# Graph network and experts on one core: the first graph layer's order, and its residual summed on TensorE

## The reference

```python
xn = layernorm(x)                                   # [3125, 256]
e = leaky_relu(el[src] + er[dst])                   # 4 heads
alpha = softmax of e over the edges of one dst
rst = segment_sum(feat_src[src] * alpha, dst) + gat_bias
h = xn + elu(rst)
graph = relu(h @ w1 + b1) @ w2 + b2                 # 256 -> 512 -> 256
mix = linear attention of xn, @ W_out + b_out
x = x + graph + mix
x = x + experts(layernorm(x), router fed with the mean over all nodes)
```

## Time and profile before

| | |
|---|---|
| runs | 2421.73, 2429.51, 2425.75 us, median 2425.75 |
| the profiled execution's own time | 2447.78 us, 0.9% over that median |
| its span in the trace | 2446.1 us |
| mean granted TensorE clock | 0.787 |
| busy in the span: PE, PEld | 1618.2, 1285.4 us |
| DVE, ACT, POOL | 1311.2, 777.3, 1128.7 us |
| most costly groups | L460 gathers 437.1 us, L1084 matmuls 330.8 us, L1020 scalings 323.0 us |

### The profile page before, as it was taken

How to read it: one execution, slowest core, us unless ns; L and a number is a source line. 1 busy time by engine, 2 the same in 40 slices (tenths; PEclk the granted TensorE clock), 3 DMA queues, 4 the chain that set the end, 5 groups by cost and what they waited for, 6 DMA issues and landing times. The chain is left out here.

```text
span 2446.1 us, 31537 instructions
## 1 busy us (share of the span) xinstructions
PE 1618.2 (66%) x8029; PEld 1285.4 (53%) x8029; DVE 1311.2 (54%) x4007; ACT 777.3 (32%) x2662; POOL 1128.7 (46%) x1255
## 2 busy tenths in 40 slices
PE   4534656655667579699897456677666666676593
PEld 3433434433344368588886335555555455565592
DVE  4722655665567758566766154444444444466344
ACT  2211744563356623256664101100100000122251
POOL 2762666666663013221213555555555555526441
PEclk8755676776668879899998687778888777787796
DMA  4751434343432073354442322222222222222586
GB/s 150 208 165 53 110 105 116 108 116 103 120 99 64 6 251 121 105 190 146 163 138 75 93 76 69 69 70 75 71 75 74 74 75 73 69 72 75 173 261 217
DMA packets 170683, 273.52 MB, mean 112 GB/s; under 512 B 28519, under 2 KB 125253, under 8 KB 170259
## 3 DMA queue, kind: packets, MB, share of 16 engines
q0 software_dynamic: 51504, 139.73, 19.9%
q1 hardware_dynamic: 76221, 88.76, 11.6%
q10 hardware_dynamic: 42790, 43.09, 5.2%
HBM read 202.27 MB, written 70.30 MB: 111 GB/s over the span
## 5 line engine op out<-in xcount | busy, mean ns | idle before, releaser
L460 POOL DMA_INDIRECT ring<-feat_d,src_lane x440 | 437.1, 994 | 276.5 <-issue 115.9
L1094 POOL DMA_INDIRECT rows<-xn_d,src_lane x440 | 427.5, 972 | 151.2 <-issue 128.0
L1084 PE MATMUL bank<-ring,a_hot 128*128 128x260 f32 x880 | 330.8, 527 | 203.2 <-DVE ring L989 93.2
L1166 PE MATMUL bank<-rows,a_hot 128*128 128x256 f32 x880 | 295.4, 447 | 165.7 <-issue 98.9
L1149 DVE TENSOR_TENSOR big<-bank,big 128x256 f32 x440 | 186.5, 424 | 345.7 <-DMA m_b<-in_L_mix_b 210.3
L1084 PEld LDWEIGHTS bank<-ring,a_hot 128*128 128x128 f32 x880 | 209.4, 257 | 286.1 <-DVE ring L989 114.6
L1020 ACT ACTIVATE ring<-ring 128x64 f32<-128x64 f32 x1320 | 323.0, 335 | 21.6 <-issue 20.4
L1166 PEld LDWEIGHTS bank<-rows,a_hot 128*128 128x128 f32 x880 | 176.1, 217 | 267.3 <-issue 250.0
L974 DVE TENSOR_TENSOR acc<-bank,acc 128x260 f32 x440 | 186.6, 424 | 137.2 <-PE bank L1084 56.5
L1953 ACT ACTIVATE x_mid<-bank,x_b 128x128 f32<-128x128 f32 x200 | 54.5, 381 | 379.2 <-remote 375.3
L1984 PE MATMUL bank<-x_lnT,big 128*128 128x128 f32 x800 | 109.8, 278 | 81.8 <-issue 81.8
(11 more groups left out here) (385 smaller groups left out, 2945.6 us busy)
## 6 DMA issues: line engine op xcount, KB each, us to landing
slots_d<-fold ACTq DMA_DIRECT2D x25, 1300.0 KB, 5.5
e_w_now<-in_L_ffn_w SPq DMA_DIRECT2D x56, 256.0 KB
a_dst_bc<-dst_lo_d SPq DMA_DIRECT2D x23, 512.0 KB
big<-in_L_ffn_W SPq DMA_DIRECT2D x16, 512.0 KB
e_x<-slots_d SPq DMA_DIRECT2D x56, 130.0 KB
ring<-feat_d,src_lane POOLq DMA_INDIRECT x440
rows<-xn_d,src_lane POOLq DMA_INDIRECT x440
e_ys<-y_d SPq DMA_DIRECT2D x24, 256.0 KB
```

The source lines that it names most:

```text
L460: pool.indirect_dma_start(ring[:, q % RING, at, :], None, table, bass.IndirectOffsetOnAxis(ap=src_lane[:, n:n + 1], axis=0)).then_inc(gath ...
L1084: pe.matmul(bank[at][:, 0:D + H], hot[:, q % HOTS, at, :], ring[:, q % RING, at, :], start=True, stop=True)\
L1094: pool.indirect_dma_start(rows[:, n % RING1, :], None, table, bass.IndirectOffsetOnAxis(ap=src_lane[:, n:n + 1], axis=0)).then_inc(gathere ...
L1166: pe.matmul(bank[s % 4][:, 0:D], hot[:, n % HOTS, :], rows[:, n % RING1, :], start=True, stop=True)\
```

## The change

In `first_aggregate` the mixer's output is made beside the steps. After the matmuls and the look-up of every fourth step TensorE sums for one tile g, in bank[3]: xT_in @ fold (two matmuls), the biases b2 and b_out (a row of ones by two rows), and the identity by x_in, that is x itself. One step later ScalarE copies the bank to `x_in`, and SP stores it to `base_d`, a new tensor in DRAM. SP loads xT and x for each tile, two tiles ahead. The steps' own sums now go round banks 0 to 2 (`n % BANKS`, BANKS = 3), and a matmul waits for the addition three before it.

In `first_graph_mlp` the two matmuls with fold, x plus biases, and two of three broadcast biases are gone; `base_in` is loaded in place of x and xT, and `residual` adds it straight to the MLP's result. The minimum moves to ScalarE, as Relu(-x) before Exp(-x). The sums over a tile come out of ScalarE's copy, now in two halves with an accumulated output. The stages of the pipelines have other lags and another order.

```diff
@@ -216,6 +216,7 @@
...
         xnT_d = dram("xnT_d", [T, P, D])
+        base_d = dram("base_d", [NP, D])
         x1_d = dram("x1_d", [NP, D])
@@ -241,7 +242,7 @@
...
             first_aggregate(nc, bank, const, acc, er, part_er, dst_lo_d, step_tile, src_lane, dst_lane, feat_d, ring,
-                            gathered, masks, decay, link)
+                            gathered, masks, decay, link, fold, xnT_d, A, base_d)
         big = sb("big", [P, E * (KT * DF + DF // P * D)])
@@ -253,7 +254,7 @@
...
             sums, every_b1 = sb("xn1_sums", [P, KT, T], ctx=kept), sb("every_b1", [P, E, DF // P], ctx=kept)
-            first_graph_mlp(nc, A, hold, bank, const, acc, fold, xnT, A["x"], xn_d, xnT_d, x1_d, xn1_d, sums, every_w1,
+            first_graph_mlp(nc, A, hold, bank, const, acc, xnT, xn_d, base_d, x1_d, xn1_d, sums, every_w1,
                             every_w2, every_b1)
@@ -802,10 +803,13 @@
...
-def first_aggregate(nc, bank, const, acc, er, part_er, dst_lo_d, step_tile, src_lane, dst_lane, feat_d, ring, gathered, masks, decay, link):
+def first_aggregate(nc, bank, const, acc, er, part_er, dst_lo_d, step_tile, src_lane, dst_lane, feat_d, ring, gathered, masks, decay, link, fold,
+                    xnT_d, A, base_d):
...
     Q = 4
+    BANKS = 3
+    EVERY = 4
     HOTS = 4
@@ -826,7 +830,15 @@
...
         loaded, hot_ready, looked_up, er_taken = S.sems("loaded", 2), S.sem("hot_ready"), S.sem("looked_up"), S.sem("er_taken")
+        xT_in, x_in, mix_ps = S.sb("xT_in", [P, 2, D]), S.sb("x_in", [P, 2, D]), bank[3][:, 0:D]
+        biases, biases_in = S.sb("biases", [2, D]), S.sem("biases_in")
+        xT_loaded, mix_stored = S.sems("xT_loaded", 2), S.sems("mix_stored", 2)
+        mix_done, mix_ready = S.sem("mix_done"), S.sem("mix_ready")
         block = S.block()
+        def mix_tile(q, late):
+            g = (q - late) // EVERY
+            return g if q >= late and (q - late) % EVERY == 0 and g < T else None
@@ -866,12 +878,36 @@
...
         def _(sp):
-            for u in range(UP_FIRST, NS // UP, 2):
+            def broadcast(u):
                 w, n = (u - UP_FIRST) // 2, min(2, NS // UP - u)
...
                   .then_inc(loaded[w % 2], 16)
+            def load(g):
+                once(sp, mix_stored[g % 2], 16 * (g // 2))
+                sp.dma_start(xT_in[:, g % 2, :], xnT_d[g, :, :]).then_inc(xT_loaded[g % 2], 16)
+                sp.dma_start(x_in[:, g % 2, :], rows_of(A["x"], g)).then_inc(xT_loaded[g % 2], 16)
+            def store(g):
+                sp.wait_ge(mix_ready, g + 1)
+                sp.dma_start(rows_of(base_d, g), x_in[:, g % 2, :]).then_inc(mix_stored[g % 2], 16)
+            late = range(UP_FIRST, NS // UP, 2)
+            for n, name in enumerate(("L0_gnn_b2", "L0_mix_b_out")):
+                sp.dma_start(biases[n:n + 1, :], A[name]).then_inc(biases_in, 16)
+            for g in range(2):
+                load(g)
+            for n in range(T + 1):
+                if n < len(late):
+                    broadcast(late[n])
+                if n > 0:
+                    store(n - 1)
+                if n > 0 and n + 1 < T:
+                    load(n + 1)
+            for n in range(2):
+                sp.wait_ge(mix_stored[n], 16 * len(range(n, T, 2)))
@@ -971,7 +1007,7 @@
...
                 to = acc[:, bass.ds(tiles[q % 2][at], 1), :].rearrange("p a n -> p (a n)")
-                dve.tensor_tensor(to, bank[at][:, 0:D + H], to, ALU.add).then_inc(added, 1)
+                dve.tensor_tensor(to, bank[n % BANKS][:, 0:D + H], to, ALU.add).then_inc(added, 1)
@@ -1019,6 +1055,10 @@
...
                     last.then_inc(last_ready, 1)
+                g = mix_tile(q, 1)
+                if g is not None:
+                    act.wait_ge(mix_done, g + 1)
+                    act.activation(x_in[:, g % 2, :], mix_ps, ACT.Copy).then_inc(mix_ready, 1)
@@ -1080,11 +1120,21 @@
...
                     pe.wait_ge(last_ready, n + 1)
-                    once(pe, added, n - Q + 1)
-                    pe.matmul(bank[at][:, 0:D + H], hot[:, q % HOTS, at, :], ring[:, q % RING, at, :], start=True, stop=True)\
+                    once(pe, added, n - BANKS + 1)
+                    pe.matmul(bank[n % BANKS][:, 0:D + H], hot[:, q % HOTS, at, :], ring[:, q % RING, at, :], start=True, stop=True)\
                       .then_inc(summed, 1)
...
                     look_up(look_up_at(b, q, 0))
+                g = mix_tile(q, 0)
+                if g is not None:
+                    pe.wait_ge(xT_loaded[g % 2], 32 * (g // 2) + 32)
+                    if g == 0:
+                        pe.wait_ge(biases_in, 32)
+                    once(pe, mix_ready, g)
+                    for k in range(KT):
+                        pe.matmul(mix_ps, xT_in[:, g % 2, k * P:(k + 1) * P], fold[:, k, :], start=(k == 0), stop=False)
+                    pe.matmul(mix_ps, const[0:2, C_ONE:C_ONE + P], biases[:, :], start=False, stop=False)
+                    pe.matmul(mix_ps, ident, x_in[:, g % 2, :], start=False, stop=True).then_inc(mix_done, 1)
@@ -1202,7 +1252,7 @@
...
-def first_graph_mlp(nc, A, hold, bank, const, acc, fold, xn1T, x_d, xn_d, xnT_d, x1_d, xn1_d, sums, every_w1, every_w2,
+def first_graph_mlp(nc, A, hold, bank, const, acc, xn1T, xn_d, base_d, x1_d, xn1_d, sums, every_w1, every_w2,
                     every_b1):
@@ -1210,37 +1260,33 @@
...
         w1, w2, b1 = S.sb("w1", [P, KT, DF]), S.sb("w2", [P, FT, D]), S.sb("b1", [P, FT])
-        bias = S.sb("bias", [P, 3, D])
-        x_in, xn_in, xT_in = S.sb("x_in", [P, R, D]), S.sb("xn_in", [P, R, D]), S.sb("xT_in", [P, R, D])
+        bias = S.sb("bias", [P, D])
+        base_in, xn_in = S.sb("base_in", [P, R, D]), S.sb("xn_in", [P, R, D])
         share, rst, low, high = (S.sb("share", [P, H]), S.sb("rst", [P, R, D]), S.sb("low", [P, R, D]),
...
         hT_ps, mid_ps, y_ps, xT_ps = ([bank[2 * n], bank[2 * n + 1]] for n in range(4))
...
         def _(sp):
-            for n, name in enumerate(("L0_gnn_gat_bias", "L0_gnn_b2", "L0_mix_b_out")):
-                sp.dma_start(bias[:, n, :], A[name].broadcast_to([P, D])).then_inc(bias_in, 16)
+            sp.dma_start(bias[:, :], A["L0_gnn_gat_bias"].broadcast_to([P, D])).then_inc(bias_in, 16)
...
                 g = i * R + j
-                once(sp, y_done, g - R + 1)
                 once(sp, x1_ready, g - R + 1, hold)
-                sp.dma_start(x_in[:, j, :], rows_of(x_d, g)).then_inc(loaded[j], 16)
+                sp.dma_start(base_in[:, j, :], rows_of(base_d, g)).then_inc(loaded[j], 16)
                 sp.dma_start(xn_in[:, j, :], rows_of(xn_d, g)).then_inc(loaded[j], 16)
-                sp.dma_start(xT_in[:, j, :], xnT_d[bass.ds(g, 1), :, :].rearrange("a p n -> p (a n)"))\
-                  .then_inc(loaded[j], 16)
@@ -1276,32 +1322,30 @@
...
-            pipeline(pool, [(5, store_xn), (4, store_x)])
+            pipeline(pool, [(6, store_xn), (5, store_x)])
...
         def _(dve):
-            dve.wait_ge(bias_in, 48)
-            dve.tensor_tensor(bias[:, 1, :], bias[:, 1, :], bias[:, 2, :], ALU.add).then_inc(bias_ready, 1)
-            dve.wait_ge(bias_ready, 1)
+            dve.wait_ge(bias_in, 16)
...
                 g = i * R + j
-                link = Steps(dve, a_step, g, 4)
+                link = Steps(dve, a_step, g, 3)
                 sums = tile_of(acc, g).rearrange("p (h d) -> p h d", h=H)
...
                                        share[:, :].unsqueeze(2).broadcast_to([P, H, DH]), ALU.mult))
-                link(dve.tensor_tensor(rst[:, j, :], rst[:, j, :], bias[:, 0, :], ALU.add))
                 link.end()
-                dve.tensor_scalar(low[:, j, :], rst[:, j, :], 0.0, None, ALU.min).then_inc(low_ready, 1)
+                dve.tensor_tensor(rst[:, j, :], rst[:, j, :], bias[:, :], ALU.add).then_inc(rst_ready, 1)
...
                 dve.wait_ge(low_exp, g + 1)
-                dve.wait_ge(loaded[j], 48 * i + 48)
+                dve.wait_ge(rst_ready, g + 1)
+                dve.wait_ge(loaded[j], 32 * i + 32)
                 link(dve.scalar_tensor_tensor(out=high[:, :], in0=rst[:, j, :], scalar=0.0, in1=low[:, j, :],
@@ -1310,12 +1354,10 @@
...
                 g = i * R + j
-                link = Steps(dve, c_step, g, 1)
                 once(dve, x1_stored[j], i * 16)
-                link(dve.tensor_tensor(x1[:, j, :], x_in[:, j, :], bias[:, 1, :], ALU.add))
-                link.end()
+                dve.wait_ge(loaded[j], 32 * i + 32)
                 dve.wait_ge(y_done, g + 1)
-                dve.tensor_tensor(x1[:, j, :], y_ps[j % 2][:, 0:D], x1[:, j, :], ALU.add).then_inc(x1_ready, 1)
+                dve.tensor_tensor(x1[:, j, :], y_ps[j % 2][:, 0:D], base_in[:, j, :], ALU.add).then_inc(x1_ready, 1)
                 dve.wait_ge(x1_ready, g + 1)
@@ -1325,20 +1367,16 @@
...
-            def sum_x(i, j):
-                g = i * R + j
-                dve.wait_ge(xn1T_ready, g + 1)
```

(33 more changed lines are left out.)

## The result

Seventeen runs each on the chips of the first measurement: before 2425.87 us (2417.56 to 2434.6), after 2437.21 us (2427.12 to 2457.22), ratio 1.0057 with a 95% interval of 1.0042 to 1.0072. The forecast was 2418 with a chance of 0.32 for slower; the time lies in the range (2396 to 2456) and on the wrong side.

What follows compares the result with a forecast made beforehand. It took the aggregation as paced by a cadence of gathers with no engine full, and the MLP stage as bound by TensorE and VectorE, both full. Aggregation +22 and MLP stage -30 gave -8 us, 2418 us, range 2396 to 2456.

Steps and rivals of the forecast that it cites:

- 3 + 5 + 2 - 1 = 9: MLP stage's early tiles: bias wait 3 us, exponential waits 5, expert-weight loads 2 saved; extra starting turn costs 1.
- The steps behind the last gathers: Aggregation: three mixes after the last gathers have nothing to hide them, 6 us more.
- 10 for the 22 mixes and 6 for the banks: Aggregation: half a microsecond for each of 22 mixes, 10 us rounded; three banks instead of four, 6 us more.
- The price of a mix: Aggregation, TensorE: eight matmul records per mix take 1.89 us at the full clock, 3.84 at the half.
- rival 2: Aggregation chain TensorE, VectorE, TensorE pays mixes at the slow clock: 60 us more there, whole +30, 2456; chance 0.28.
- The step that called ScalarE's wait free before 766 us: Aggregation: ScalarE runs whole steps ahead, so waiting to copy each mix costs nothing before 766 us.
- higher clock: Aggregation: TensorE activity lifts the granted clock, lowering the upper bound by 49 us at most.
- I carry the difference over as it is: Whole kernel: the -8 us sum of stage changes is applied unchanged to the median 2425.75, giving 2417.8.
- signs of being wrong: Wrong if the aggregation grows by more than 40 or less than 10 us, or the MLP stage shrinks under 20.
- Rival 1: Aggregation: the cadence of gathers swallows the mixes; only the last three cost, 6 us; whole -24, 2402; chance 0.27.
- the cadence: Aggregation: gathers go on until their slots run out, and TensorE's results are seen late until then.
- Rival 3: MLP stage gives only half, ScalarE or expert weights binding it first: -15 + 22 = +7, 2433; chance 0.09.

Runs made afterwards that it cites:

- exp_first: before with ScalarE's exponential put first in its MLP-stage turn, not last; slower kind of chip: 2420.5 us, 0.9978 of before.
- g1_only: before with after's MLP-stage reordering, mixer's matmuls, x and biases kept there, old aggregation; 0.9953 to 0.9958 on faster chips, 0.9982 on the slower kind (g1_only_4).
- double_mix: after with the four matmuls of each mix done twice; slower kind of chip: 2483.0 us, 1.0237 of before.
- before_again: The kernel before, unchanged, profiled again; faster kind of chip: 2070.4 us, ratio 0.9996.

## Why the prediction was wrong

**The MLP stage: right.** 30 us, and by the steps named. From the last addition to tile 9's elu it takes 55.3 us in place of 67.1 (12 less; 3 + 5 + 2 - 1 = 9 were forecast), from there to tile 24's elu 61.5 in place of 78.7 (17; 18), and the tail 17.1 in place of 17.9 (1; 3). A turn is 4.04 us (4.05 forecast), 4.35 us of the bias wait are gone and both waits for the exponential. exp_first alone takes 9.4 us out of the stage, 5.5 of them before tile 9 (5 were said), 4.4 in the fifteen steady turns; its tail is 0.7 longer. g1_only_4 takes 11.3. It still waits 9.45 us for three biases, and its TensorE turn is 966.65 - 961.84 = 4.81 us:

```profile
961.84 0.38 PE L1371 MATMUL bank<-const,g_h 128*128 128x128 f32 x2
...
966.65 0.38 PE L1371 MATMUL bank<-const,g_h 128*128 128x128 f32 x2
```

The other 19 us down to after's 133.4 are the mixer's matmuls (0.77 a turn), with the operation for x and biases, and 4.6 us of the bias wait; no run parts these.

**The aggregation: right in size, its terms less so.** +22.4 against before's trace, +22 to +29 and 25.7 in the mean against all three. The steps behind the last gathers cost 9 to 10 us and not 6 (93.3 in place of 83.4, 83.9 and 84.1 from the last gather's end to the last addition). The stretch up to there grew by 12 to 20 us, where 10 for the 22 mixes and 6 for the banks were said. The price of a mix was set too low (1.89 and 3.84 us; 2.19 and 4.14 measured), and the 1.4 us a mix from which rival 2 was to decide left tail and banks out: with these 12 us in the 30 it is 18 / 22 = 0.8. (The step every 5.9 us while gathers run is 6.0 by the earlier trace rows.) The step that called ScalarE's wait free before 766 us is doubtful: by the timeline above it is paid at least once, and TensorE's weight loads wait 80.5 us in 59 cases for ScalarE's scalings, against 39.5, 49.8 and 51.2 in about 30 in the three traces without mixes. How much of that lengthens the stage is not shown.

The prediction allowed the mixes to pay part of their price by a higher clock. The Trainium skill (TensorE: Matmul & The Clock Gate, What's actually happening) says that activity releases the throttle. On the faster kind the granted clock of the stage goes that way, from 0.80 and 0.82 to 0.89 in both traces of after. On the slower kind it hardly does: while gathers run it is 0.74 with mixes and 0.73 and 0.74 without; only before's own trace has 0.70. Nothing of the price came back there: the steps' own matmuls were busy 330.2 us in after, 330.8 in the earlier trace rows, 311.7 and 315.3 in the other two.

**The step that failed is "I carry the difference over as it is".** It takes the sum of two stages, read off one execution, for the difference of two medians, and so puts everything else at nothing: where that execution lies among the runs, and all other stages. Before's profiled execution lay 22 us above its median, outside all of its 17 runs, and its mean granted clock of 0.787 is under that of all 33 runs of before on the three other chips of this kind (0.789 to 0.801). Of the 22 us about 10 lay in a stage that the change doesn't touch: the second aggregation was 762.9 us, and 752.3, 753.0 and 754.5 in three others; the first one was some 5 over the mean of the two others.

Forecast were -8 us, measured +11.3. Of the 19 between them 4 are the aggregation (+25.7 against three traces, +22 forecast), some 6 are the second aggregation of after (759.0 against 753.3 in the mean of the three others, forecast at nothing), and 4 are the place of after's profiled execution under its median. The last 5 have no place. They don't seem to be the mixes': g1_only_4 and exp_first, which have none, lack as much, with an MLP stage 11.3 and 9.4 us shorter than before's and medians only 5.8 and 4.5 us lower (on the faster kind g1_only's stage gives about 10 us and the whole 9). Both are set against the one trace of before, though, whose stage may have been long. Whether after's longer second aggregation is chance or a rule, one trace can't say; double_mix holds the whole change and has 753.0. So the cause of these parts stays open. What can be said is that stage sums from one execution each carry 10 to 20 us of such variation here, and the forecast was 8. None of the prediction's signs of being wrong showed it: the aggregation grew by between 10 and 40 us, and the MLP stage shrank by more than 20.

**Rival 2 (slower, the mixes paid at the slow clock)** has the right sign and the wrong size, a stage growth of 60 against 22 to 29. The second 25 mixes cost about what it says of the first; by which chain, no run shows. **Rival 1 (swallowed)** is near what happens on the faster kind, -17 to -20 us for its -24, though by waits for landing gathers and not by the cadence that I described; on the slower kind double_mix speaks against it. **Rival 3** is refuted: 4.04 us a turn. My claim that no step waits for a gather holds on the slower kind alone.

Which version to take: on the faster kind after with four banks is the fastest met that computes the whole result (0.9876, with the late copy 0.9887 and 0.9886), ahead of both kernels though of after only narrowly. On the slower kind g1_only (0.9982) and exp_first (0.9978) are the only ones below before.

## What to carry to other kernels

Before a forecast of a fraction of a per cent is built on one profiled execution, look at where that execution stands in the runs, and take the unchanged stages' lengths from more than one trace: their variation is the floor of what a sum of stage differences can say. Work moved under a loop that seems to have slack is hidden only up to the slack, and doubling it is a quick way to see how much was left: here the first set cost 0.9 to 1.2 us a piece and the second 2.3. Moving a matmul out of a full stage into such a loop is a bet on what bounds the loop, and that can differ from chip to chip.

## What the runs showed of the hardware

The same program took 2425 to 2428 us on three chips and 2069 to 2075 on five. The difference lies in the stages in which GpSimd gathers: first aggregation 620 against 513 us, second 753 to 763 against 541, the mixer's context stage 84.4 against 39.5 (the next stage starts 18 us later there, so 28 us are left), the second layer's mixer before its aggregation 63 against 32 (the next stage starts 19 us later there, so 14 us are left). The MLP stage and the experts are alike (163.7 and 160.6 to 164.4; 297 to 301). The longest waits of the mixer's stage, before on the slower kind:

```profile
DVE er L720 <- DMA xnT_d<-ring: 50.8, 2, 28.8
ACT m_ek L757 <- remote: 41.5, 4, 20.6
```

and before_again on the faster:

```profile
DVE er L720 <- PE bank L766: 19.7, 8, 3.1
ACT m_ek L757 <- PE bank L779: 18.0, 21, 2.5
```

The longest of them in the timelines of PE and DVE of before:

```profile
180.72 1.22 PE L766 MATMUL bank<-part_er,m_dst_hot 128*128 x8
...
201.15 0.26 DVE L720 TENSOR_REDUCE er<-bank 128x32 f32<-128x96 f32 x1 [28.79 <-DMA xnT_d<-ring]
203.67 0.26 DVE L720 TENSOR_REDUCE er<-bank 128x32 f32<-128x96 f32 x1 [1.87 <-PE bank L766]
```

By TensorE's row the look-up was done at 181.94, and VectorE took it 19 us later, after the stage's last gather (issued until 194.7); the next one it took within 0.1 us of its end. On the faster kind no such wait is over 3.1 us. In the first aggregation an addition starts 3.0 us in the mean after the end of its matmul in before (3.3 while gathers run, 1.6 behind the last) and 1.5 us in before_again, and the gathers themselves are equally long (1002 and 1006 ns a piece). So on the slower kind results are taken late while gathers run. That this is what makes those chips slower is argued from it, and why some chips have it and others not wasn't found.
